# Two attention layers on one core: the shift of the softmax is cut on GpSimd instead of VectorE, and placed by transfers in both halves of the first stage

## The reference

```python
q = Wq @ x + bq            # 16 x 1024
k = Wk @ x + bk            # 16 x 1024
v = Wv @ x + bv            # 128 x 1024
attn = softmax(q.T @ k)    # 1024 x 1024, over the last axis
out = gamma * (v @ attn.T) + x
```

## Time and profile before

| | |
|---|---|
| median of 3 runs | 213.25 us (212.74 to 218.13) |
| the profiled execution's own time | 212.72 us |
| its span, first to last instruction | 210.9 us |
| PE busy | 187.4 us, 89% |
| mean granted clock of TensorE | 0.984 |

### The profile page before, as it was taken

One profiled execution on the slowest core, in us unless ns is written; L12 is line 12 of the kernel. 1 busy time (PEld: TensorE's weight loads), 2 busy tenths in 40 slices (PEclk: granted clock), 3 DMA queues, 4 the chain that ended last, 5 costly groups with the idle time before them and its releaser, 6 DMA issues.

```text
span 210.9 us, 3123 instructions
## 1 busy us (share of the span) xinstructions
PE 187.4 (89%) x1107; PEld 121.6 (58%) x1109; DVE 168.8 (80%) x162; ACT 153.3 (73%) x219; POOL 149.1 (71%) x95
## 2 busy tenths in 40 slices
PE   7999959699994999899969999499995999799983
PEld 2453437464673667664747568276673777456751
DVE  0269896888899698979997889959999867894991
ACT  2268865998994988798977889398884788858400
POOL 1494061507998599959995999989999078784930
PEclk9999996999999999999999999999998899999999
DMA  6907040000210003000400030001310001000211
GB/s 166 364 17 177 22 103 2 0 3 3 51 50 2 6 0 99 3 3 0 101 3 3 0 78 26 0 3 53 99 50 0 33 23 50 3 5 14 86 49 51
DMA packets 3871, 9.49 MB, mean 45 GB/s; under 512 B 545, under 2 KB 913, under 8 KB 3857
## 3 DMA queue, kind: packets, MB, share of 16 engines
q1 hardware_dynamic: 3856, 9.30, 14.9%
HBM read 2.89 MB, written 2.10 MB: 24 GB/s over the span
## 4 chain that ended last, share of the span: by engine, by line
PE 61%; DVE 21%; ACT 7%; issue 4%; POOL 3%; DMA 2%; SPq 0%; DVEq 0%; POOLq 0%
PE out_psum L692 25%; PE out_psum L690 5%; PE ring L667 5%; PE ring L619 5%; PE ring L643 5%; ACT ring L433 5%; DVE shift_parts L542 5%; PE ring L629 5%; DVE attn_lo L519 5%; DVE shift L539 4%; PE out_psum L693 3%; PE out_psum L726 3%; DVE shift_parts L544 3%; DVE x_all L567 2%; DVE neg_max L524 2%
## 5 line engine op out<-in xcount | busy, mean ns | idle before, releaser
L524 DVE TENSOR_REDUCE neg_max<-ring 128x1 f32<-128x1024 f32 x64 | 76.1, 1220 | 17.5 <-PE ring L645 17.1
L433 ACT ACTIVATE ring<-ring,neg_max 128x1024 f32<-128x1024 f32 x64 | 69.6, 1087 | 19.6 <-DVE neg_max L524 19.5
L346 POOL TENSOR_TENSOR attn_lo<-attn,attn_hi 128x1024 fp32r<-128x1024 f32 x34 | 81.9, 2418 | 2.6 <-ACT attn_hi L451 1.8
L445 ACT ACTIVATE attn<-ring 128x1024 f32<-128x1024 f32 x64 | 63.7, 1025 | 15.5 <-PE ring L669 13.1
L341 POOL TENSOR_SCALAR attn_hi<-attn 128x1024 fp32r<-128x1024 f32 x35 | 39.1, 1124 | 39.8 <-ACT attn L445 36.0
L643 PE MATMUL ring<-qk_swapped,qk 64*128 64x512 f32 x56 | 26.6, 481 | 3.0 <-ACT ring L433 2.4
L669 PE MATMUL ring<-qk_swapped,qk 64*128 64x512 f32 x64 | 28.0, 467 | 0.0
L667 PE MATMUL ring<-qk,qk_swapped 64*128 64x512 f32 x64 | 27.6, 461 | 0.3 <-DVE shift_rows L553 0.2
L645 PE MATMUL ring<-qk,qk_swapped 64*128 64x512 f32 x56 | 27.0, 488 | 0.0
L693 PE MATMUL out_psum<-attn,v 64*128 64x512 f32 x56 | 26.4, 591 | 0.0
L692 PE MATMUL out_psum<-attn,v 64*128 64x512 f32 x56 | 26.4, 591 | 0.0
(11 more groups left out here) (72 smaller groups left out, 371.1 us busy)
## 6 DMA issues: line engine op xcount, KB each, us to landing
qk_swapped<-qk SPq DMA_DIRECT2D x16, 256.0 KB, 3.7
out_dram<-x_all SPq DMA_DIRECT2D x8, 256.0 KB, 2.0
x_all<-x_in SPq DMA_DIRECT2D x3, 512.0 KB, 7.6
x_all<-x_in SPq DMA_DIRECT2D x2, 256.0 KB, 3.6
late<-late_in SPq DMA_DIRECT2D x1, 320.0 KB, 6.5
units<-units_in SPq DMA_DIRECT2D x1, 320.0 KB, 6.8
weights<-weights_in SPq DMA_DIRECT2D x1, 131.0 KB, 2.2
qk<-shift_rows SPq DMA_DIRECT2D x7, 8.0 KB
```

Of the source, the lines that this page charges most:

```text
L346: nc.gpsimd.tensor_tensor(attn_lo[:, k - 1], attn[:, k], attn_hi[:, k - 1].bitcast(fp32), ALU.subtract).then_inc(cut_made["lo", "gpsimd"], 1)
L433: nc.scalar.activation(e[:], e[:], ACT.Exp, bias=neg_max[s][:, i:i + 1], accum_out=row_sum[s][:, i:i + 1]).then_inc(sum_made, 1)
L445: nc.scalar.activation(attn[:, k], ring_tile("ET", s, k)[:].rearrange("p (a n) -> p a n", a=2), ACT.Exp).then_inc(attn_made, 1)
L524: nc.vector.tensor_reduce(neg_max[s][:, i:i + 1], ring_tile("E", s, i)[:], axis=AX.X, op=ALU.max, negate=True).then_inc(max_made, 1)
```

## The change

The three small operations on the shift (`parts`) move from DVE's queue to GpSimd's, with the same waits; the copy that makes `hi` becomes a multiplication by 1 and addition of 0 there. `ADDED` is empty: half 0 of stage 0 gets its rows by transfers (`place.0.0`) as half 1 does, and the small products on the `ET` slots are gone. Stage 0 has two native slots (0 and 7), as the other stages, where it had four (0, 1, 4, 7). All five tables are new, with `hi`, `lo`, `v_hi` and `v_lo` shared out differently: GpSimd has 39 `lo`, 33 `hi` and 4 `v_lo` where it had 34, 35 and 8; DVE has 9 `lo` and 4 `v_lo` where it had 12 and none; ACT has 15 `hi` where it had 11. `warm` has 19 products instead of 14.

```diff
-NATIVES = [(0, 1, 4, 7), (0, 7), (0, 7), (0, 7), (0, 7), (0, 7), (0, 7), (0, 7)]
+NATIVES = [(0, 7), (0, 7), (0, 7), (0, 7), (0, 7), (0, 7), (0, 7), (0, 7)]
-ADDED = (0,)
+ADDED = ()
...
 POOL_ORDER = """
-mask.1.0 stack.1.0 v_lo.0.0 hi.0.2 lo.0.2 hi.0.3 lo.0.3 hi.0.6 lo.0.6 hi.0.5 v_lo.1.0 lo.0.5 hi.1.1 lo.1.1 hi.1.2
+mask.1.0 stack.1.0 parts.0.0 parts.0.1 v_hi.0.0 hi.0.1 hi.0.2 hi.0.3 lo.0.2 lo.0.3 v_hi.1.0 lo.0.1 hi.0.5 hi.0.6
...
 SP_ORDER = """
-swap.1.0 swap.0.0 swap.2.0 place.0.1 place.1.1 swap.3.0 place.2.1 swap.4.0 place.3.1 swap.5.0 place.4.1 swap.6.0
+swap.0.0 swap.1.0 place.0.0 swap.2.0 place.0.1 place.1.1 swap.3.0 place.2.1 swap.4.0 place.3.1 swap.5.0 place.4.1
...
+        def parts_of(s, h):
+            return shift_parts[s][:, 2 * tiles_of(s, h).start:2 * tiles_of(s, h).stop]
...
+            def split_shift(s, h):
+                tiles = tiles_of(s, h)
+                part, count = slice(tiles.start, tiles.stop), len(tiles)
...
+                else:
+                    hi, lo = (parts_of(s, h)[:, n * count:(n + 1) * count] for n in range(2))
+                    whole = shift[s][:, part]
+                pool.wait_ge(max_made, all_of(nth_max, s, tiles))
+                pool.wait_ge(log_made, nth_log[s, h])
+                nc.gpsimd.tensor_tensor(shift[s][:, part], neg_max[s][:, part], log_sum[s][:, part],
+                                        ALU.subtract).then_inc(shift_made, 1)
+                pool.wait_ge(shift_made, nth_parts[s, h])
+                nc.gpsimd.tensor_scalar(hi, whole, 1.0, 0.0, ALU.mult, ALU.add).then_inc(shift_hi_made, 1)
+                pool.wait_ge(shift_hi_made, nth_parts[s, h])
+                nc.gpsimd.tensor_tensor(lo, whole, hi.bitcast(fp32), ALU.subtract).then_inc(shift_cut, 1)
...
-                nc.vector.tensor_tensor(shift[s][:, part], neg_max[s][:, part], log_sum[s][:, part],
-                                        ALU.subtract).then_inc(shift_made, 1)
-                dve.wait_ge(shift_made, nth_parts[s, h])
-                nc.vector.tensor_copy(hi, whole).then_inc(shift_hi_made, 1)
-                dve.wait_ge(shift_hi_made, nth_parts[s, h])
-                nc.vector.tensor_tensor(lo, whole, hi.bitcast(fp32), ALU.subtract).then_inc(shift_cut, 1)
```

More of the change, by code:

```diff
@@ L80 @@
+hi.6.1 attn.6.2 hi.6.4 sum.7.2 attn.6.0 log.7.1 v_hi.7.0 attn.6.5 attn.6.7 hi.6.5 attn.7.3 attn.7.6 hi.7.3 attn.7.1
+attn.7.0 attn.7.2 attn.7.7 attn.7.5 attn.7.4 hi.7.4
 """
 DVE_ORDER = """
-max.0.7 max.0.3 v32.0.0 max.0.5 max.0.4 max.0.0 max.0.2 max.0.1 max.1.6 parts.0.0 max.0.6 rows.0.0 mask.2.0
-stack.2.0 parts.0.1 max.1.2 rows.0.1 max.1.1 max.1.3 max.1.5 max.1.0 max.1.4 max.1.7 max.2.7 max.2.0 max.2.5
-parts.1.1 v32.1.0 rows.1.1 max.2.2 finish.0.0 max.2.4 mask.3.0 stack.3.0 max.2.6 max.2.3 max.2.1 finish.0.1 v32.2.0
@@ L90 @@
[L90 to L91 removed]
+max.0.1 max.0.0 max.0.3 max.0.2 max.0.4 max.0.5 max.0.7 mask.2.0 max.0.6 rows.0.0 stack.2.0 max.1.6 max.1.4 v32.0.0
+rows.0.1 max.1.1 v_lo.0.0 v32.1.0 max.1.0 max.1.2 max.1.7 max.1.5 max.1.3 max.2.7 max.2.6 max.2.1 rows.1.1 max.2.3
+finish.0.0 mask.3.0 stack.3.0 max.2.4 max.2.2 max.2.0 max.2.5 finish.0.1 max.3.4 max.3.0 rows.2.1 max.3.2 max.3.5
@@ L216, in build_attention_layers @@
         nth_evac, nth_sbuf_stack = counts(ACT_USES, "evac"), counts(POOL_USES, "stack")
-        nth_v32, nth_parts, nth_rows = (counts(DVE_USES, what) for what in ("v32", "parts", "rows"))
+        nth_v32, nth_rows = counts(DVE_USES, "v32"), counts(DVE_USES, "rows")
+        nth_parts = counts(POOL_USES, "parts")
         nth_sum, nth_attn = counts(ACT_USES, "sum"), counts(ACT_USES, "attn")
@@ L404, in _ @@
                     make_v_lo(s)
+                elif what == "parts":
+                    split_shift(s, k)
                 elif what == "mask":
@@ L582, in _ @@
                     attn_lo_of(s, i)
-                elif what == "parts":
-                    cut_shift(s, i)
                 elif what == "rows":
```

108 lines of the change are left out of this document (50 added, 58 removed).

## The result

| | before | after |
|---|---|---|
| median | 215.69 us (4 runs, 212.74 to 218.13) | 201.29 us (4 runs, 198.37 to 204.03) |
| ratio after / before | | 0.934, 95% interval 0.928 to 0.940 |
| profiled execution, own time | 212.72 us | 203.89 us |
| its span | 210.9 us | 202.1 us |
| its mean granted clock | 0.984 | 0.975 |

The changed kernel is 6.6% faster; 203.5 us was forecast.

A forecast was written before the change was run, and what follows sets the result against it. PE was taken to wait for tiny DVE shift operations held by whole GpSimd instructions. From 212.7 us, 6.7 for the periods and 2.5 for the front part came off: 203.5 us, own range 200 to 207.5 (chance 0.57).

The forecast's parts named there:

- the rule that the prediction cites: DVE and GpSimd share an SBUF port pair as an exclusive lock; the later is held for the other's whole instruction.
- The price of a small GpSimd operation: Each of three shift operations on GpSimd takes 0.35 us, between bounds 0.10 and 0.69; three with hand-overs 1.3 us.
- What is late next: In the seven periods, engine loads of 19.7 to 20.0 us a stage make the period 20.6, keeping 6.7 of 10.0 us.
- The 0.45 us of slack: Before, DVE, next after PE at 21.1 us a stage, lay this far under the period of 21.55.
- Stage 0, as a number: Front part gains 2.5 us; first ET at 24.6 instead of 25.89, placement taking 3.4 us, logarithm ending at 19.5.
- The natives: Two more cut slots in stage 0: PE gains 0.8 us, GpSimd's idle time hides its added work; zero.
- The end: From the last shift product to the span's end, 28.4 us: zero change, with -1.5 and +2.5 as ends.
- The clock: Mean granted clock 0.984 costs 3.4 us over the span; part returns if waits go, left to the range.
- (a): Rival: all waits go and the clock stays up, 196 to 199 us; chance 0.15.
- (b): Rival: GpSimd becomes the bound, idling some 1.2 us a stage, period 21.2, 209 to 210 us; chance 0.17.
- (c): Rival: small GpSimd operations take 1.0 us each, nothing changes, 212 us; chance 0.05.
- (d): Rival: placement landing late holds stage 0's start, ET 5 us later, 218 us; chance 0.06.

The follow-up runs named there:

- b_parts: Kernel before with its own tables, native slots and added rows; only the three shift operations moved from DVE's to GpSimd's queue: 198.17 us, ratio 0.926.
- a_dve: Changed kernel with its tables, but the three shift operations back in DVE's queue: 218.8 us, ratio 1.010 against the kernel before.
- b_reduce: Kernel before, the middle of the three DVE shift operations written as a reduction over one element instead of a copy: 212.15 us, ratio 0.985.
- a_added: Changed kernel with half 0 of stage 0 added by PE as before, without its transfer: 204.93 us.
- b_placed: b_parts with half 0 of stage 0 placed by transfers instead of added by PE: 204.41 us.
- b_natives: b_parts with slots 1 and 4 of stage 0 cut instead of native: median 200.02 us.
- a_again: Changed kernel run again with no edit: 205.94, 204.36, 206.18 and 198.38 us.
- a_warm: Changed kernel with two more warm-up products behind each of QK.1, E.0.3 and E.0.2: 200.61 us.
- b_tail: b_parts with three attn_hi of stage 7 moved from GpSimd to ACT: 196.65 to 199.68 us in six runs, ratio 0.919.
- b_share: b_parts with five attn_lo moved from GpSimd to DVE: 200.64 us.

## Why the prediction came out right, and where it was off

**The bound and the mechanism were right, the closeness of the number was luck.** The wait of PE at the small product was 13.8 us and is 1.2; under 4 was forecast. `b_parts` and `a_dve` show from both sides that the move of the three operations makes the difference, `b_reduce` that what held them was the kind of DVE operation beside GpSimd's. That 203.5 us lies beside the 203.89 of the profiled execution comes of two misses that cancel: its start is 4.6 us later than forecast, with the clock down, and its periods are 3.5 us shorter. At a clock of 1.00 the gain is 5 us larger than forecast. Two of the first operations were held the other way round, as the rule that the prediction cites allows: L379 at 88.06 took 1.17 us beside a DVE `attn_lo` that ended at 89.15, and the one at 172.63 took 1.05. PE waited 0.48 and 0.35 us behind them.

**The price of a small GpSimd operation** was taken as 0.35 us and is 0.20. The lower of the two bounds was the better neighbour. The logarithm to product time was forecast at 2.1 us and came to 2.3 in the mean of the whole stages of after (1.1 to 3.2). But the 4.3 that it was held against is stage 2 alone: the mean of before was 3.7, so the time fell by 1.5 and not by 2.2. The waits vanished all the same, since PE has other work queued ahead of most products: at stage 2 of after the time is still 3.2 us and PE doesn't wait.

**"What is late next" was the mis-sized term.** The period was forecast at 20.6 us and measured 20.1 (19.8 in `b_parts`), which keeps 10.2 us (12.2) where I had 6.7. The loads of the engines were forecast well: GpSimd 160.1 against 159.0 measured, ACT 157.7 against 155.8, DVE 149 against 147.7. What failed was dividing them by eight stages and holding that against the period. The windows over the seven periods, before first, then after, in the columns given above:

```profile
31.58:182.46 150.88, 135.27 (x894) 93.78 (x894) 129.28 (x128) 123.27 (x179) 120.16 (x72) 0.98 0.10 26
```

```profile
33.71:174.41 140.70, 133.76 (x905) 92.82 (x904) 116.57 (x109) 128.28 (x186) 132.26 (x94) 1.00 0.10 28
```

In the periods of after GpSimd is busy 132.3 / 7 = 18.9 us each, ACT 18.3 and DVE 16.7, not 20.0, 19.7 and 18.6, since a good part of their work lies ahead of the second product or behind the last. PE with 19.1 is the next one itself. There was a microsecond of room in each period that I took for filled. The 0.45 us of slack came from the same division and was too small: inside the periods of before the next engine after PE, DVE, was busy 129.3 / 7 = 18.5 us of 21.55. So a load taken too high and a slack taken too low partly cancelled; in after the period stands 1.0 us above PE and 1.2 above GpSimd. `b_parts` at 138.7 us lies even under the 139.4 that the prediction gave for PE without its waits, although 3.9 us of waits for the parts are left in that run. Up to 3 us of the gain in the periods are the clock, 0.98 in the window of before and 1.00 there; the sum had left them to the range.

**Stage 0, as a number, was about right, and by its steps wrong.** Forecast was a second product 2.5 us earlier. `a_dve`, which has the tables of after and kept its clock in stage 0, has it at 29.00, 2.6 earlier; the logarithm, forecast to end at 19.5, ends at 20.0 there:

```profile
19.82 0.19 ACT L466 ACTIVATE log_sum<-row_sum 128x4 f32<-128x4 f32 x1
...
21.30 0.23 PE L681 MATMUL ring<-units,shift_parts 128*8 128x128 f32 x1
...
27.07 0.50 PE L693 MATMUL ring<-qk,qk_swapped 64*128 64x512 f32 x1
```

But the first ET comes at 27.07, not 24.6, and later than the 25.89 of before. The prediction followed the transfer's way (3.4 us) and left out what the listing of PE's order ahead of it shows between the small product and the ET: 5.8 us, nearly all of it queued work. And `b_parts` has its second product at 29.07 without any of it. In `b_parts` the gain in stage 0 is the wait of 2.34 us ahead of the second product, now gone. For the placement a gain of 1.3 us at the first ET was forecast, and no run shows one: without it the changed kernel has its first ET at the same time (32.38 and 32.27, clock down in both, `a_added`), and with it the old tables lose 2 to 3.4 us, the clock apart (`b_placed`).

**The natives** were costed at zero because GpSimd waits in stage 0. They cost about 1 us with the old tables (`b_natives`), so not all of the idle time was cover; probably because the four operations queue ahead of those of stage 1.

**The end** was taken as zero and is 0.7 us, inside its bounds.

**The clock** was left to the range, as a gain. It was both: the two dips of before are gone and a new one stands in stage 0 of the profiled execution; two of six executions, and three of four in `a_again`, had a mean clock of 0.975 or less. It is worth 5 to 8 us: the spread between the executions at 1.00 and the others, `a_again` included. Perhaps it is the 16-row score products one behind another in the new table that allow it (`a_warm` points there); why it happens in one execution and not in the next stays open. `b_tail`, with the start of `b_parts`, shows that the old tables aren't free of it.

**The rivals.** (a), all waits gone and the clock up at 196 to 199 us, is about what the executions at a clock of 1.00 did, with 198.4 to 199.8; it had 0.15, and the argument against it was the division by eight. The profiled run and the median lie in the forecast's own range of 200 to 207.5. (b), GpSimd as the bound, didn't occur as priced: its idle time ahead of the parts is 1.3 us in all seven periods, not 1.2 in each, and the period is 20.1 and not 21.2. It is nearly as full as PE there (132.3 us of 140.7 against 133.8), but in `b_parts` five `attn_lo` less on it made the kernel slower (`b_share`). (c) fell with 0.20 us an operation. (d), a start held by the placement, did not occur: in after PE is busy right up to the first ET, and `a_added` starts no earlier.

## What to carry to other kernels

When an in-order engine that everyone waits for waits itself for a tiny operation, look at what that operation shares with its neighbour: moved to the engine that held it, or written as a kind that isn't held, it costs 0.2 us. The second way has to take in the whole chain, since the stall passes to the next operation that can be held (`b_reduce`). Try such an edit alone in the old order before planning everything anew; here the plan around it added nothing. And hold loads against a period only after counting them inside that period, since a page's busy time divided by the number of stages, or an engine's share of the chain, can name bounds that aren't there.
